# Six decoder blocks on one core: a position select on GpSimd for the score mask, kernel rows through DRAM, and another order of the steps

## What is computed

```python
scores = jnp.einsum('bqhd,bkhd->bhqk', qq, kk) * scale
causal = jnp.tril(jnp.ones((S, S), dtype=bool))
scores = jnp.where(causal[None, None], scores, jnp.finfo(scores.dtype).min)
probs = jax.nn.softmax(scores, axis=-1)
y = jnp.einsum('bhqk,bkhd->bqhd', probs, v).reshape(B, S, H)
```

## Time and profile before

| | |
|---|---|
| median of 3 runs | 501.48 us (497.2, 501.48, 502.75) |
| the profiled execution | 500.73 us, of which the span of the trace is 498.9 |
| mean granted TensorE clock | 0.931 of full |
| PE busy | 418.0 us, 84% of the span |
| DVE busy | 335.4 us, 67% |
| ACT busy | 301.0 us, 60% |
| POOL busy | 123.9 us, 25% |

### The profile page before, as it was taken

How to read it: one execution, slowest core, us unless ns; L and a number is a source line. 1 busy time by engine, 2 the same in 40 slices (tenths; PEclk the granted TensorE clock), 3 DMA queues, 4 the chain that set the end, 5 groups by cost and what they waited for, 6 DMA issues and landing times.

```text
span 498.9 us, 5938 instructions
## 1 busy us (share of the span) xinstructions
PE 418.0 (84%) x2047; PEld 205.3 (41%) x2049; DVE 335.4 (67%) x616; ACT 301.0 (60%) x512; POOL 123.9 (25%) x129
## 2 busy tenths in 40 slices
PE   6979869778979999979865984657689899999994
PEld 3444423343335554434322331324466544544441
DVE  1487865679877842836888997968975553554453
ACT  3646786515246679897887884545338488722443
POOL 1100370000420054058647574435020000000000
PEclk9989998969999999989986987768979999999999
DMA  8940000554190000022036667588500000000000
GB/s 266 354 155 6 1 2 0 172 80 147 62 188 10 3 3 1 2 74 96 0 107 186 182 197 220 137 211 240 227 0 1 1 0 1 0 1 0 1 21 21
DMA packets 23470, 42.13 MB, mean 84 GB/s; under 512 B 6950, under 2 KB 12295, under 8 KB 22279
## 3 DMA queue, kind: packets, MB, share of 16 engines
q1 hardware_dynamic: 23332, 41.66, 28.5%
q10 hardware_dynamic: 108, 0.10, 0.1%
HBM read 36.67 MB, written 4.72 MB: 83 GB/s over the span
## 4 chain that ended last, share of the span: by engine, by line
PE 58%; DVE 19%; ACT 6%; issue 5%; POOL 4%; DMA 4%; SPq 2%; DVEq 0%; ACTq 0%; POOLq 0%
PE PS L894 7%; PE PS L899 6%; PE PS L921 6%; DVE AR L1514 6%; ACT AR L1172 4%; PE PS L822 4%; PE PS L808 4%; DVE AR L1835 4%; POOL AR L2152 3%; PE PS L658 3%; PE PS L791 3%; DVE AR L1520 2%; PE PS L666 2%; DMA AR<-scan 2%; PE PS L1025 2%
## 5 line engine op out<-in xcount | busy, mean ns | idle before, releaser
L1172 ACT ACTIVATE AR<-PS 128x512 f32<-128x512 f32 (+2 forms) x185 | 98.2, 561 | 92.4 <-PE PS L894 39.6
L1514 DVE TENSOR_TENSOR AR<-PS,AR 128x512 f32<-128x512 f32 (+1 forms) x120 | 80.0, 678 | 58.0 <-PE PS L899 28.9
L1172 ACT ACTIVATE AR<-AR 128x256 f32<-128x256 f32 (+3 forms) x110 | 47.1, 462 | 50.0 <-DVE AR L1514 35.6
L2152 POOL TENSOR_TENSOR AR<-AR 128x512 f32<-128x512 f32 (+2 forms) x48 | 53.0, 1113 | 95.8 <-DVE AR L1514 59.4
L1168 ACT ACT_TABLE_LOAD x49 | 62.9, 1283 | 1.6 <-PEq L2484 0.7
L1523 DVE TENSOR_REDUCE stats<-PS 128x1 f32<-128x128 f32 (+4 forms) x88 | 43.5, 525 | 10.1 <-PE PS L794 7.0
L1835 DVE TENSOR_TENSOR_SCAN AR<-PS,AR 128x512 f32<-128x512 f32 x32 | 38.8, 1213 | 5.6 <-ACT PS L1172 5.6
L658 PE MATMUL PS<-AR,W_sq 128*128 128x256 f32 x88 | 26.9, 413 | 13.1 <-ACT AR L1172 8.6
L2238 POOL TENSOR_TENSOR RR<-KL,lags 128x512 f32<-128x512 f32 x24 | 26.6, 1143 | 39.9 <-PE PS L811 39.9
L791 PE MATMUL PS<-RR 97*128 97x512 bf16 (+3 forms) x128 | 31.4, 318 | 4.6 <-DVE stats L1523 2.4
L1172 ACT ACTIVATE PS<-AR,RA 128x512 f32<-128x512 f32 x32 | 21.6, 686 | 17.1 <-DMA AR<-scan 9.5
(11 more groups left out here) (238 smaller groups left out, 729.6 us busy)
## 6 DMA issues: line engine op xcount, KB each, us to landing
AR<-scan SPq DMA_DIRECT2D x64, 256.0 KB, 3.9
RR<-in_ffn SPq DMA_DIRECT2D x1, 2688.0 KB, 12.1
RR<-in_ones SPq DMA_DIRECT2D x2, 832.0 KB
RR<-in_ones SPq DMA_DIRECT2D x2, 784.0 KB
RA<-in_moe SPq DMA_DIRECT2D x1, 1539.5 KB, 6.3
W_mla<-in_mla SPq DMA_DIRECT2D x1, 1504.0 KB, 14.0
W_late<-in_late SPq DMA_DIRECT2D x1, 1076.0 KB, 11.8
RA<-in_xa SPq DMA_DIRECT2D x1, 1056.0 KB, 7.6
```

The lines of the kernel that those rows point to most:

```text
L1172: nc.scalar.activation(out_, in_, func, bias=bias, scale=scale).then_inc(*done("act", *step))
L1514: nc.vector.tensor_tensor(out_, a, b_, op).then_inc(*done("dve", *step))
L2152: nc.gpsimd.tensor_tensor(out_, a, b_, op).then_inc(*done("pool", *step))
```

## The change

It has four parts.

1. The mask product of the score units (811) is gone. Instead POOL goes over the exponentials in place and sets those of forbidden positions to zero (`affine_select`): four instructions per group of heads, each on four diagonal blocks of 128 by 128, 32 instructions in all. The selections of a group wait for its exponentials 3, 7, 7 and 9, and the stages of `values` wait for the selections instead of the exponentials. The ten exponential slots are now adjacent (6 to 15 of `AR`), the copy `yc` is in slot 5. The mask product of the maxima (794) stays.
2. `Ksb` goes to `Kdl` by way of DRAM: four DMAs out (64 KB each, in 128 bytes pieces), one back in (256 KB), in place of the 16. Between them SP issues the spread of one more scan unit.
3. New `TURNS` for PE, DVE, ACT and POOL.
4. New `TABLES`: 43 loads of ACT tables in place of 49; in the last stage 12 in place of 18, with one before the last layer norms of both batches in place of one inside them.

```diff
-    "pool": [*SPLIT, "dx", *[f"by{i}" for i in _N]],
+    "pool": [*SPLIT, *[f"am{g}.{i}" for g in range(GROUPS) for i in range(4)], "dx", *[f"by{i}" for i in _N]],
...
-        P = [[AR[b][:, i, :] for i in (5, 7, 8, 9, 10, 11, 12, 13, 14, 15)] for b in range(B)]
+        P = [[AR[b][:, i, :] for i in range(6, 16)] for b in range(B)]
...
             sp.wait_ge(*after("act", "w", "kp1"))
-            for a in range(PA):
-                sp.dma_start(Kdl[:, PB_ * a:PB_ * a + PB_],
-                             Ksb[a:128:32, :].rearrange("p (d l) -> p d l", l=PB_)).then_inc(kshuf, 16)
-            spread_rows(1, 6, NS)
+            for q in range(4):
+                place = kernel_dram[32 * q:32 * q + 32, :].rearrange("d (a l) -> a d l", l=PB_)
+                sp.dma_start(place, Ksb[32 * q:32 * q + PA, :].rearrange("a (d l) -> a d l", l=PB_))\
+                    .then_inc(kdraft, 16)
+            spread_rows(1, 6, 7)
+            sp.wait_ge(kdraft, 16 * 4)
+            sp.dma_start(Kdl, kernel_dram).then_inc(kshuf, 16)
+            spread_rows(1, 7, NS)
             load("ffn1", tiles["ffn1"])
             load("sel1", tiles["sel1"])
...
-                    mm(ring[:, c:c + n_], Kst[b][0:KROWS, h, 128 * kb:128 * kb + 128], Qst[b][0:KROWS, h, 128 * kb:T],
-                       start=(c == 0), stop=False)
-                masked = [c // 128 for _, _, c in segs]
-                mm(blocks(ring, masked), w("bf", "id"), over(w("bf", "mT"), [128, len(masked), 128], 1), start=False,
-                   stop=True).then_inc(*done("pe", b, f"su{n}"))
+                    last = mm(ring[:, c:c + n_], Kst[b][0:KROWS, h, 128 * kb:128 * kb + 128],
+                              Qst[b][0:KROWS, h, 128 * kb:T], start=(c == 0), stop=(c == segs[-1][2]))
+                last.then_inc(*done("pe", b, f"su{n}"))
 
             def values(b, g, stage):
-                pe.wait_ge(*after("act", b, f"su{g * UNITS + {0: 3, 1: 7, 2: 9}[stage]}"))
+                pe.wait_ge(*after("pool", b, f"am{g}.{(0, 2, 3)[stage]}"))
                 if stage == 0 and g:
                     pe.wait_ge(*after("act", b, f"yc{g - 1}"))
...
-                    last = tr(own(b, 0)[:, 128 * t:128 * t + 128], A(b, 6)[:, 128 * t:128 * t + 128], w("sq", "id"))
+                    last = tr(own(b, 0)[:, 128 * t:128 * t + 128], A(b, 5)[:, 128 * t:128 * t + 128], w("sq", "id"))
...
-                pe.wait_ge(kshuf, 16 * PA)
+                pe.wait_ge(kshuf, 16)
...
-                        f(A(b, 6), own(b, 2), ACT.Copy, (b, f"yc{g}"))
+                        f(A(b, 5), own(b, 2), ACT.Copy, (b, f"yc{g}"))
...
+                zero = pool.to_reg(0.0)
+                for g in range(GROUPS):
+                    for i, (units, step, at, last) in enumerate(((6, T, 0, 3), (10, T, 0, 7), (10, T, 384, 7), (14, 256, 0, 9))):
+                        pool.wait_ge(*after("act", b, f"su{g * UNITS + last}"))
+                        blocks = grid(flat(b, units, units + 4 * step // T), step)[:, :, at:at + 128]
+                        nc.gpsimd.affine_select(blocks, blocks, [[0, 4], [1, 128]], ALU.is_ge, zero, base=0,
+                                                channel_multiplier=-1).then_inc(*done("pool", b, f"am{g}.{i}"))
+                        yield
...
-        "w39 b6 w13 a1 w2 a1 w1 a9 w1 a4 b1 a2 b16 w1",
+        "w39 b6 w1 a9 b3 a1 b1 a2 b1 a1 b3 a3 w1 b1 w1 b3 w2 b1 w2 b3 w7 a1 w2 a3 w1 a10 b1 a3 b16 w1",
```

More of the change, by code:

```diff
@@ L345, in build @@
                    for i in range(AHEAD[k])}
+        kernel_dram = nc.dram_tensor("kernel_rows", (D, T), F32, kind="Internal").ap()
+        kdraft = ctx.enter_context(nc.semaphore("kernel_rows_written"))
         kshuf = ctx.enter_context(nc.semaphore("kernel_rows_moved"))
```

## The result

| | before | changed |
|---|---|---|
| median | 499.53 us (20 runs) | 501.65 us (20 runs) |
| lowest and highest | 493.57, 502.75 | 498.69, 507.21 |
| profiled execution | 500.73 us, span 498.9 | 500.74 us, span 499.0 |

The ratio is 1.0083, 95% interval 1.0047 to 1.0118. It is that of the means, over the runs that were not in the chip's slower state, so it isn't the quotient of the medians. The forecast was 491.5 us. The two profiled executions are equal within 0.1 us, so what the traces differ by is where time went, not how much there was. A single difference of 2 to 4 us between two traces is therefore no proof; the experiments' ratios decide.

A forecast was written before the change was run, and what follows sets the result against it. It took PE to bound the attention and last stage, DVE the experts and scans: 500.73 - 3.2 - 4.5 - 1.2 - 1.0 = 490.8 us, plus 0.75 for the median, 491.5 us; range 480 to 505.

The forecast's parts named there:

- The attention, -7.6 us, by "PE full": Attention, 142 to 213 us: PE is full, so less PE work saves time; batch 1 comes 7.6 us early.
- The last selection ends near 216, `mo` near 221.3: End of attention: 44.7 us of POOL work from about 171 ends near 216, batch 1's output product 5.5 us later.
- Mask products, 7.4 us off PE: Attention scores: removing 80 mask products takes at most 7.4 us off PE's stream.
- A selection, 1.1 us: POOL in the attention: each select over 512 elements per partition takes 1.1 us, between 0.6 and 2.2.
- DVE beside POOL, 0 us: Attention: POOL's new work does not slow DVE; 0 us, bounds 0 and +3.
- `dl` of batch 0, +4 us, net -3.2 with the attention: Behind the attention: batch 0's scan starts 4 us later, DVE loses 4.4; net -3.2 us, bounds -10 and +4.
- Kernel rows, -4.5 us: Scans, 326 to 338 us: rows through DRAM let the seventh spread issue sooner; -4.5 us, bounds 0 and -6.
- `ed.s`, -1.2 us: After the scans: this 1.93 us step leaves batch 0's chain, moved behind batch 1's layer norm; -1.2 us, bounds 0 and -1.9.
- Table load in the last chain, -1.0 us: Program's end: the 1.28 us table load moves ahead of both batches' last norms; -1.0 us, bounds 0 and -1.3.
- no change: Whole kernel: a measurement within about 1%, 5 us, of the kernel before; chance 0.19.
- the order gives the gain back: Rival, behind the attention: batch 0's scan starts 8 us later, DVE idles throughout; about 496 to 497 us, chance 0.17.

The follow-up runs named there:

- e3: The changed kernel (new order throughout, rows through DRAM) with the mask products back on PE and no selections on POOL; ratio 1.0061 to the kernel before.
- h1: The kernel before with rows through DRAM, masks on PE and the new order only up to batch 0's score units; ratio 0.9833.
- h2: h1 with the new order kept to the end of batch 1's attention, the old order from there; ratio 1.0065.
- k1: h1 with the selections of both batches on POOL in place of the score units' mask products; ratio 1.0059.
- k3: h1 with the score units' mask products left out and nothing in their place, so it computes something else; ratio 0.9732.
- h3: h2 with the new order kept to the end of batch 1's scan, the old order from there; ratio 1.0129.
- e1: The kernel before with only the kernel's rows sent through DRAM, old order and masks on PE; ratio 0.9907, 4.6 us faster.
- m2: The same program as k4, run again with more rounds; ratio 0.9782 to the kernel before.
- k4: h1 with the new order and table loads again from the end of batch 1's scan to the program's end; ratio 0.9814.

## Why the prediction was wrong, step by step

- **The attention, -7.6 us, by "PE full".** This is the step that failed. The prediction took PE as full from 142 to 213 and so 7 us of its work as 7 us of time ("PE alone would allow more", 216), and let only POOL take some of it back. That PE is full was a property of the old order, which had batch 1's maxima as filler between batch 0's waits; the change used them up early. The new order was priced only at `dl`, and the attention was taken as a pool of work. Measured: `mo` of batch 1 ends at 226.3, and at 227.9 in e3, which has no selection; from h1 to h2 the attention's order costs 11.6 us, the largest term of all, for which the sum had nothing.
- **"The last selection ends near 216, `mo` near 221.3".** It added up POOL's durations as if it were never idle and never in the wrong place. Measured: the last selection ended at 218.4, although each is 0.45 us shorter than assumed. POOL was busy 24.09 of 33 us from 180 to 213. In an in-order list what decides is what stands ahead of each selection when its exponential is there, not the sum (k1: 8.2 us of waiting on PE with an idle POOL in between). This step was wrong too, but it isn't what `mo` at 226.3 comes from, as e3 shows.
- **Mask products, 7.4 us off PE.** The stream's price was an upper bound and used as one. Their absence is worth 5.0 us in h1's order (k3).
- **A selection, 1.1 us.** Mis-sized: 0.654. The nearest row (0.575 for a fill) was the better guide than the two-input products that I chose. The Trainium skill (GPSIMD Engine Reference, section 3.1, Elementwise) has 1.03 cycles an element for a body of at most two operations and about 2.6 for a two-input `tensor_tensor`, at the engine's 1.2 GHz (section 1) an estimated 0.44 and 1.1 us for 512 elements. The select's 0.654 lies between the two, the products' 1.14 to 1.26 are near the second.
- **DVE beside POOL, 0 us.** Right for the whole, wrong in the place. Four products of batch 0's routing took 4.55 us in place of 1.42, beside POOL's products, not its selections. But DVE waited for PE behind them: 3.95 us, and 6.92 in e3, where they were fast. The rule of the Trainium skill that I had weighed (GPSIMD Engine Reference, sections 1 and 8: shared SBUF interfaces) holds with that number.
- **`dl` of batch 0, +4 us, net -3.2 with the attention.** `dl` was to end at 258.3 and ended at 263.8, +9.6. Of the 5.5 us between, 5.0 are there at the second cast of batch 1's routing (261.4, forecast 256.4), as much as `mo` was later than forecast; so this term was right and took over the attention's error. The step from h2 to h3 prices it alone: `dl` 5.8 us later, the first scan 3.0, the whole 3.2 by ratio, where I had 4.4. From `mo` of batch 1 to its scan unit 5 the changed kernel loses 9.4 us, against the 4.4 of the sum.
- **Kernel rows, -4.5 us.** Right: -4.8 between units 5 and 6, -4.6 alone (e1).
- **`ed.s`, -1.2 us.** Not contradicted: from scan unit 15 to the layer norm 7.1 us in place of 8.6. Over all traces it takes 7.1 to 7.5 us in six of the seven kernels with the new order at the end, and 8.6 to 9.7 in the nine with the old. The seventh, m2, has 9.4 and is the same program as k4 (7.5), so 1 to 2 us are likely and not shown.
- **Table load in the last chain, -1.0 us.** Wrong. The changed kernel has 42 loads in all (not 43, as the section on the change says), and the load is gone from the chain, but from batch 1's input to the end the stage is 0.4 us longer, and its last expert product ends 0.87 us later (492.95 against 492.08). What was late next was PE, which is full in the last stage (115.10 of 118 us).
- **Not foreseen:** the 6.5 us of lead up to the first score unit, about 3 us by h1 and within the noise there.
- **The range.** The bounds of the terms do not add up to 486 and 496, but to about 482 and 505, and 508 with DVE's +3. That the measured 501.65 us lies between 480 and 505 is the width of the range and no merit of the sum: it belongs to "no change", which had 0.19.

The rival "the order gives the gain back" had 0.17 and came nearest. It was half right: batch 0's scan does start later by about what it said (first scan instruction +6.8 us, it had 8), but it kept the attention's 7.6 us, of which 2.6 came, and so arrived at about 496.

## What to carry to other kernels

An engine that is full is full in that order: before you price an order, ask which work waits for nobody, and whether it still lies beside the work that waits. Moving an operation to an idle engine puts it between its producer and its consumer; on an in-order engine its price is its own length plus whatever stands ahead of it. Here 0.65 us on an idle GpSimd, between producer and consumer, won nothing against 0.05 to 0.12 us of a full TensorE. When a step moves, look at what it will run beside. And a step that has become slow is a cause only if nothing else would have held its successor: the kernel without the suspect (here e3) tells.

## What the hardware showed

- A select by position on GpSimd, in place on four blocks of 128 columns, takes 0.654 us by mean; a two-input product of the same 512 elements 1.14 to 1.26.
- A VectorE product of 196 columns with two SBUF inputs goes from 0.36 us to between 1.10 and 1.18 beside a two-input product on GpSimd, about the length of GpSimd's own instruction. A reduction with one input beside the selections keeps its 0.36.
- An issue on SyncE takes about 0.6 us whether the DMA has 16 KB (0.59 each by the earlier trace rows) or 64 KB in pieces of 128 bytes (0.49 to 0.71); 64 KB in such pieces land in 3.5 us. Fewer, larger DMAs were cheaper for the queue here even by way of DRAM.
